# A graph layer on one core: edge groups of one tile instead of two, and padding entries that point to 128 zero rows

## The reference, cut to what matters

```python
N, C, HEADS, E = 6250, 256, 4, 206250      # nodes, features, heads, edges with self loops
xn = layernorm(x)
Wh = (xn @ W.T + b).reshape(N, HEADS, 64)
alpha_src, alpha_dst = einsum(Wh, a_src), einsum(Wh, a_dst)          # (N, HEADS)
e = leaky_relu(alpha_src[src] + alpha_dst[dst])                      # one per edge and head
ex = exp(e - segment_max(e, src)[src])
gnn = segment_sum(ex / segment_sum(ex, src)[src] * Wh[dst], src)     # over each node's edges
x = x + gnn + mix(xn)          # linear attention over all nodes, two layer norms, a GELU layer
out = x + ffn(layernorm(x))    # a shared MLP and two of four experts, by a softmax gate
```

## Time and profile before

| | us |
|---|---|
| median of 3 runs | 3117.58 |
| lowest and highest | 3114.31, 3119.29 |
| the profiled execution's own time | 3118.8 |
| its span, first to last instruction | 3117.0 |
| PE matmul busy | 2181.7 (70%) |
| POOL busy | 2160.0 (69%) |
| DVE busy | 1882.2 (60%) |
| ACT busy | 792.2 (25%) |
| mean granted TensorE clock | 0.847 of full speed |

### The profile page before, as it was taken

The page is one execution under the profiler, slowest core; times in us unless marked ns, Lnnn a source line. Parts: engine busy times, 40 slices in busy tenths (PEclk is TensorE's granted clock), DMA queues, the critical chain, the costliest instruction groups (busy, mean ns, idle before and its releaser), DMA issues.

```text
span 3117.0 us, 40701 instructions
## 1 busy us (share of the span) xinstructions
PE 2181.7 (70%) x10817; PEld 1529.3 (49%) x10818; DVE 1882.2 (60%) x3946; ACT 792.2 (25%) x1396; POOL 2160.0 (69%) x2141
## 2 busy tenths in 40 slices
PE   1001984177778787787977879778778787787877
PEld 0000552155555555555655556555555555555554
DVE  8998552265664656666566664656655656666463
ACT  6000442022222222222222222222222222222222
POOL 1008777677777777777777777777777777777770
PEclk6555997588989988989889898889989988989988
DMA  6000221434344444444444444444444444444462
GB/s 188 0 0 13 75 74 41 96 101 119 96 103 124 102 111 116 104 123 103 115 110 104 122 102 124 102 103 123 102 106 124 102 117 108 105 123 103 123 91 29
DMA packets 271584, 306.05 MB, mean 98 GB/s; under 512 B 164258, under 2 KB 210856, under 8 KB 271080
## 3 DMA queue, kind: packets, MB, share of 16 engines
q0 software_dynamic: 97760, 251.60, 30.9%
q1 hardware_dynamic: 140098, 18.08, 3.9%
q10 hardware_dynamic: 33480, 33.36, 3.4%
HBM read 276.25 MB, written 26.62 MB: 97 GB/s over the span
## 4 chain that ended last, share of the span: by engine, by line
PE 50%; DVE 14%; issue 8%; POOL 6%; ACT 2%; DMA 1%; ACTq 0%; DVEq 0%; POOLq 0%; SPq 0%; another core or an unknown queue 0%
PE sum_banks L1027 26%; PE f_banks L1042 9%; POOL gathered L965 6%; DVE onehot L1430 5%; PE turned L999 3%; PE f_banks L1161 2%; DVE gathered L1451 2%; PE f_banks L1086 1%; PE sum_banks L1015 1%; PE f_banks L1067 1%; PE f_banks L1162 1%; DVE he L1579 1%; DVE he L1582 1%; PE f_banks L1068 1%; ACT onehot_t L1202 1%
## 5 line engine op out<-in xcount | busy, mean ns | idle before, releaser
L965 POOL DMA_INDIRECT gathered<-table,col x1872 | 1898.4, 1014 | 572.9 <-issue 563.2
L1027 PE MATMUL sum_banks<-gathered,onehot 128*128 128x260 f32 x3744 | 1070.5, 449 | 105.7 <-DVE gathered L1451 104.4
L1027 PEld LDWEIGHTS sum_banks<-gathered,onehot 128*128 128x128 f32 x3744 | 824.8, 226 | 298.1 <-issue 133.0
L1451 DVE TENSOR_TENSOR gathered<-gathered 128x512 f32<-128x512 f32 x936 | 591.4, 692 | 50.6 <-ACT gathered L1206 47.8
L1430 DVE TENSOR_TENSOR onehot<-iota_row,col 128x1024 f32<-128x1024 f32 x236 | 288.9, 1225 | 448.4 <-PE sum_banks L1027 448.0
L290 POOL DMA_INDIRECT edge_list<-payload,pos x244 | 249.9, 1024 | 293.4 <-DVE pos L411 216.5
L1202 ACT COPY onehot_t<-turned 128x1024 bf16<-128x1024 bf16 x236 | 238.6, 1011 | 332.5 <-PE turned L999 330.2
L1216 ACT COPY acc<-sum_banks x234 | 87.8, 375 | 915.4 <-PE sum_banks L1027 700.0
L999 PE MATMUL turned<-ident_bf,onehot 128*128 128x128 bf16 x1888 | 157.7, 231 | 165.6 <-DVE onehot L1430 165.5
L999 PEld LDWEIGHTS turned<-ident_bf,onehot 128*128 128x128 bf16 x1888 | 115.3, 103 | 183.7 <-DVE onehot L1430 145.6
L1009 PE MATMUL scores<-t,onehot_t 128*128 x1880 | 100.1, 175 | 122.0 <-DVE scored L1439 82.0
(11 more groups left out here) (322 smaller groups left out, 2564.0 us busy)
## 6 DMA issues: line engine op xcount, KB each, us to landing
gathered<-table,col POOLq DMA_INDIRECT x1872
xn_batch<-xn ACTq DMA_DIRECT2D x13, 512.0 KB, 4.3
x_all<-in_x SPq DMA_DIRECT2D x1, 6144.0 KB
x_batch<-in_x ACTq DMA_DIRECT2D x12, 512.0 KB
out<-xf ACTq DMA_DIRECT2D x12, 512.0 KB
edge_list<-xn_all SPq DMA_DIRECT2D x2, 2176.0 KB, 14.1
edge_list<-payload,pos POOLq DMA_INDIRECT x244
col<-edge_list SPq DMA_DIRECT2D x236, 8.0 KB, 2.1
```

The source lines that it names most:

```text
L965: g.indirect_dma_start(gathered[:, l, t, :], None, sh["table"], bass.IndirectOffsetOnAxis(ap=col[l][:, t // G, t % G, 0:1], axis=0)).then_ ...
L1027: last = t.matmul(sum_banks[:, ds(banks_of[g], 1), 0:TB].rearrange("p a w -> p (a w)"), onehot[:, l % 3, g * G + k, :], gathered[:, l, g * ...
L1451: v.tensor_tensor(value, value, gathered[:, l, tiles, C:TB].unsqueeze(3).broadcast_to([P, G, H, HD]), ALU.mult).then_inc(s_mul, 1)
```

## The change

- `G` is 1 and `GROUPS` is 8: a lot is still 8 tiles and an iteration 48, but a group is one tile, so a block is rounded up to 128 entries instead of 256. `GROUPS_MAX`, `NG`, `BLK_COLS`, `LOT_WORDS` (now 10) and `LIST` follow from it. The entries of one tile lie in the list one behind the other, so `col` is loaded in pieces of one entry (8 bytes) instead of two.
- The products on DVE stay four of two tiles; PE waits for them at every second tile.
- `blk` and `lots` are two partitions of one tensor, `tables`, so that they take the room of one.
- `table` has 128 rows of zeros from `NO_TARGET` on. The padding entries inside the runs point to row `NO_TARGET` plus their own partition (`own_row`), those of the list to `NO_TARGET` plus their position modulo 128.
- Several buffers of stage one move into memory whose contents are no longer used (`late`, `pads`), and DVE and ACT wait for `s_filled` before their turns.

```diff
-G = 2
+G = 1
 GR = G * P
-GROUPS = 4
+GROUPS = 8
+PAIRS = G * GROUPS // 2
...
+        own_row = sb("own_row", [P, 1], I32)
...
-            sp.dma_start(sh["table"][NO_TARGET:NO_TARGET + 1, :],
-                         x[0:1, NB:NB + 2, :].rearrange("p b c -> p (b c)")[:, 0:TB]).then_inc(s_zero_row, 16)
+            sp.dma_start(sh["table"][NO_TARGET:NO_TARGET + P, :],
+                         x[:, NB:NB + 2, :].rearrange("p b c -> p (b c)")[:, 0:TB]).then_inc(s_zero_row, 16)
...
-            g.memset(pad_rows[:, :, 0].bitcast(I32), NO_TARGET).then_inc(s_fill, 1)
+            cycles = LIST // (2 * P) // P
+            g.iota(pad_rows[:, 0:cycles * P, 0].bitcast(I32), [[0, cycles], [1, P]], base=NO_TARGET,
+                   channel_multiplier=0).then_inc(s_fill, 1)
+            g.iota(pad_rows[:, cycles * P:, 0].bitcast(I32), [[1, LIST // (2 * P) - cycles * P]], base=NO_TARGET,
+                   channel_multiplier=0).then_inc(s_fill, 1)
...
                 step(v.tensor_scalar(words, words, NO_TARGET >> 7, 7, ALU.bitwise_or, ALU.logical_shift_left))
+                step(v.tensor_tensor(words, words, own_row[:, :].broadcast_to([P, words.shape[1]]), ALU.bitwise_or))
...
                 for g in range(GROUPS):
-                    pe.wait_ge(s_mul, n * GROUPS + (g + 1))
+                    if g * G % 2 == 0:
+                        pe.wait_ge(s_mul, n * PAIRS + (g * G // 2 + 1))
                     for k in range(G):
...
-            def product(it, l, g):
+            def product(it, l, pair):
-                tiles = slice(g * G, g * G + G)
+                tiles = slice(pair * 2, pair * 2 + 2)
...
-                for g in range(GROUPS):
-                    product(it, l, g)
+                for pair in range(PAIRS):
+                    product(it, l, pair)
...
+        tables = sb("tables", [2 * 32, NG // GROUPS * LOT_WORDS], I32)
...
-            "blk": sb("blk", [1, NG], I32),
-            "lots": sb("lots", [1, NG // GROUPS, LOT_WORDS], I32),
+            "blk": tables[32:33, 0:NG],
+            "lots": tables[0:1, :].rearrange("a (l w) -> a l w", w=LOT_WORDS),
```

More of the change, by code:

```diff
@@ L76 @@
 assert TE + PAD_SLOTS <= SLOTS and WINDOWS == PART_ENDS[-1] and GR % Q == 0
-assert NO_TARGET == 52 * P and NB * P <= 1 << 13 and NO_TARGET < 1 << 13
+assert NO_TARGET == 52 * P and NO_TARGET + P <= 1 << 13 and NB * P <= 1 << 13 and NO_TARGET < 1 << 13
 assert NB <= NBK < P
@@ L539, in _ @@
             dve.wait_ge(s_bias_out, 1)
+            dve.wait_ge(s_filled, 32)
             all_turns(dve, turn)
```

23 lines of the change are left out of this document (13 added, 10 removed).

## The result

| | before | after |
|---|---|---|
| median of the comparison, us | 3118.43 (4 runs) | 3241.37 (4 runs) |
| ratio, 95% interval | | 1.0394 (1.0356 to 1.0432) |
| span of the profiled execution, us | 3117.0 | 3236.8 |
| mean granted TensorE clock | 0.847 | 0.81 |

The kernel became **3.9% slower**. The forecast of 3085 us and the range up to 3140 were wrong, and so was the direction. An iteration was dropped as counted, 55 us by my own price, so about 178 us were added to the rest of the loop.

A forecast was written before the change was run, and what follows sets the result against it. It took the consumers (PE, DVE, ACT) to set the pace already, 1.2 us a segment behind POOL. From the profiled execution, 3118.8 - 55 + 27 + 2 - 6.5 - 1.5 = 3085 us, range 3056 to 3140.

The forecast's parts named there:

- One iteration fewer, -55 us: Loop: smaller groups end the planner at iteration 38 instead of 39, saving 48 gathers and 55 us of consumers' time.
- The consumers set the pace, so additions show in full: Loop: PE, DVE and ACT need 191.1 us a segment, POOL 189.9, so work added to their chain shows fully.
- Longer register loads, +27 us: PE's record load of nine words: 920 ns even, 1570 odd, +0.33 us each, mainly in plain iterations; +27 us in all.
- rival A: Odd records loaded word by word, 2232 ns, +0.99 us in odd lots; 3124 us in all; chance 0.33.
- The clock: PE's sums after a longer pause: a lower clock could carry rival A beyond 3130 us; no separate term.
- In heavy lots it is mostly covered: Record load in lots with dense matmuls or sums waiting for DVE: only 0.4 us left uncovered there.
- The block table's eight words: PE's load ahead of the scores: two fours, +0.33 us, hidden by a 1.13 us wait for DVE.
- address instructions +2 us: PE's queue: eight more a lot at 46 ns, hidden except about 0.2 us a segment where scores start late.
- 128 zero rows, -6.5 us: Last lots' gathers: pads read different rows, so DVE's 6.51 us wait for the last gather should go.
- List in pieces of 8 bytes, no cost: Column loads: 1024 pieces instead of 512, but asked for an iteration ahead, so no cost.
- Before the loop: -1.5 us: Stages before the loop: +0.9 us for or-ing in pad rows, less a shorter trial sweep; together -1.5 us.
- The rule of the Trainium skill: Register loads at some 200 ns per register: four added words cost 0.8 us every lot, sum near 3137 us.

The follow-up runs named there:

- b_early8: Kernel before with records every 32 bytes and both register loads issued earlier in PE's order: 3143.1 us, ratio 1.0078.
- a_fill: Changed kernel with PE doing the eight transposes of each odd lot three times over: 3225.4 us, ratio 1.0357 to before.
- b_load9: Kernel before with PE loading nine words of the record table instead of five, using the first five: 3213.6 us, ratio 1.0312.
- a_stride12: Changed kernel with a record every 48 bytes instead of 40, all aligned to 16: 3124.5 us, ratio 1.0013 to before.
- a12_pairs: Changed kernel with 48-byte records, both tiles of a pair sharing block and bank (four address instructions, not eight): 3084.6 us, ratio 0.9907.
- a_split_early: Changed kernel with bank numbers in 32-byte records, ACT's two numbers in their own table, both loads early: 3085.5 us, ratio 0.9899.

## Why the prediction was wrong

*One iteration fewer, -55 us: the count was right.* 1824 gathers, 38 iterations. With both causes of the loss taken out 3068 us are left, where 3063 would be this term alone; b_early8 shows that part of this closeness is luck.

*The consumers set the pace, so additions show in full: right,* and more strongly than I used it. DVE's waits for gathers went to nothing.

*Longer register loads, +27 us: the step that failed first.* "Even: 590 + 332 = 920 ns": measured 847. "No row separates these two; I take the first": it was the second, 2184 ns, word by word, rival A. By the rule I took, four of the nine words would have been aligned and fetched at once; the chip does that only if the record as a whole begins aligned. The even record was mis-read too: four aligned words cost 332 ns, five and eight both 590, nine 847, so it is each begun group of four words that adds some 258, and not each single word. But A's own sum was 3124, and the load's part alone cost 117 us, so the price of the word was not the whole error.

*The clock: missed.* I wrote that PE's lower clock "would carry this case beyond 3130", with no number on it, though the earlier trace rows held one: 4.96 against 3.77 us. In a plain iteration the sums of its first five lots went from 20.0 us (4.96 and four times 3.77) to 27.3 (6.80, 6.47, 3.77, 6.49, 3.77), +7.2 us; the pauses before the zeros added 3 x 0.94 + 3 x 0.26 = 3.6. Together that is 10.8 where the iteration grew by 10.5: **some two thirds of it are clock** (which includes the slower head that the scores bring). Over the whole kernel the two are even: the sums went from 4.57 to 5.01 us a lot, 99 us in 228 lots, and the pause before the zeros from 0.42 to 0.86, 100 us. Together that is more than the 175 that were added, as PE's waits for DVE became shorter. a_fill shows the clock by itself: with PE kept at work the sums lost 97 us.

*"In heavy lots it is mostly covered": about right for the record's load, wrong for the change.* b_load9, which has the long load alone, adds 1.3 us to the heavy iterations of a segment (150.5 to 151.8). But with the change they grew by 5.3, to 155.8, and in a_stride12, where odd records load like even ones, they still take 155.0. Most of that is the address instructions: in a12_pairs these iterations take 151.1.

*"The block table's eight words ... +0.33 us, ahead of the scores, where PE then waits 1.13 us for DVE: hidden", and address instructions +2 us: wrong.* That wait comes after the scores and hides the load only where the scores come early. Where they are themselves what is late (the wait of 82.0 us for DVE in 50 times, in the trace of before), the load stands behind the wait: +0.27 us, and eight address instructions make the scores 0.46 us longer. I had bounded them by 46 ns each; between matmuls as short as these each added 0.115 us. Measured: 33 us by the address instructions (a12_pairs), and 22 more by the early loads on top of it, both by the ratios. One figure of that term was also off in the working: at 3.77 us a lot two tiles of sums are 0.94 us, not 0.87.

*128 zero rows, -6.5 us: nothing measurable.* The transfer got shorter as argued, but the wait belonged to the balance between POOL and the consumers, and I had just shifted that by 27 us in another term. A gain that is read off a wait must be taken off again if the same sum makes the waiting side slower.

*List in pieces of 8 bytes, no cost: not tested by itself,* but nothing speaks against it: of POOL's 709.3 us of pauses before gathers 540.5 are the gaps that nothing released and 168.5 the waits for sums, so none is left for a column load.

*Before the loop: -1.5 us.* The first lot's scores were weighed at 612.1 us after and 612.2 before in this kernel's two profiles: about nothing.

*The rule of the Trainium skill.* "Runtime: NRT & Kernel Launch", section on instruction fetch mechanics, gives some 200 ns per register even for bulk. Here an odd record costs 243 ns a word, an even one 94. So it comes near for the odd half of the records and not for the others; these loads are from SBUF, while the page speaks of loads from HBM. It gave 3137 us, on the right side of no change and still 104 short, since the load's own length was one term of three.

## What to carry to other kernels

Before changing the size of a record that an engine loads into registers, look at its stride: keep it a multiple of 16 bytes (8 past one was the slow case here; other offsets weren't tried), and put the load ahead of the waits and not behind them, but not ahead of work that covers it. It pays only where the loading engine sets the pace: the kernel before, bound by POOL, gained nothing. Price a pause of PE with the matmuls behind it at half speed, from the trace, before calling a longer pause small. And an instruction between matmuls is only hidden where the matmuls are long; ask it of the shortest ones, at the places where PE comes late.

## What was not expected of the hardware

**A register load depends on where its bytes begin.** PE, from SBUF: four aligned words 332 ns, five 590, eight 590, nine 847; five words 8 bytes past a multiple of 16 took 1242 and nine 2184.

**A gather on POOL that meets a long DVE operation takes longer.** Most gathers take 0.946 to 0.949 us, in every kernel here. In a_split_early, POOL and then DVE:

```profile
1868.84 0.94 POOL L978 DMA_INDIRECT gathered<-table,col  x1 [0.30 <-issue]
1870.08 1.88 POOL L978 DMA_INDIRECT gathered<-table,col  x1 [0.30 <-issue]
1872.27 0.94 POOL L978 DMA_INDIRECT gathered<-table,col  x1 [0.30 <-issue]
```

```profile
1869.92 1.23 DVE L1447 TENSOR_TENSOR onehot<-iota_row,col 128x1024 f32<-128x1024 f32 x1 [1.31 <-PE sum_banks L1043]
1871.06 2.53 DVE L1468 TENSOR_TENSOR gathered<-gathered 128x512 f32<-128x512 f32 x4
```

The gather that begins inside the one-hot takes twice as long; the one that begins inside the products does not. Counted over all gathers, what they took over 0.946 us each is 127 us in the kernel before, of which 107 in gathers that overlap a DVE operation of over 1 us; 158 and 138 in b_early8; 169 and 147 in a_split_early. Of a_split_early's gathers 178 of the 232 that begin inside a one-hot are stretched by over 0.1 us, and of the 745 that overlap no DVE operation of 0.6 us or more, one. The Trainium skill, "GPSIMD Engine Reference", section on specifications, says that GpSimd's SBUF interfaces are shared with VectorE, with contention where a DVE instruction has two SBUF inputs. The one-hot and the products have two. The trace agrees for the one-hot, and far less for the products: of the 431 gathers that begin inside one and overlap no longer operation, 42 are stretched. This stretching is in POOL's pace, and I had taken 1.321 us as a constant of POOL. No run changed DVE's operations alone, so the cause is argued from what overlaps. Why quicker consumers place more one-hots on gathers isn't shown: their phase to POOL differs, and no run changed that alone.

**Filler work keeps the clock but not the time** (a_fill): 116 us of transposes brought 97 us off the sums and 16 off the whole, the granted clock up from 0.81 to 0.843.
